# A transformer step on one core: choices and ranks moved in the last three steps, early loads, expert weights rounded in a ring of four

## The reference

```python
# x: 64 images of 2 x 104 x 104; 169 tokens of 128 features per image
y = conv(normed, W, strides=(8, 8)); y = y.reshape(B, E, -1).transpose(0, 2, 1)
...
q_prime = exp(q @ proj.T); k_prime = exp(k @ proj.T)        # 8 heads, 64 features
context = einsum('bhmf,bhmd->bhfd', k_prime, v)
out = einsum('bhnf,bhfd->bhnd', q_prime, context) / (q_prime @ k_prime.sum()  + 1e-6)
...
topv, topi = top_k(x @ Wg, 2); w = softmax(topv)            # 2 of 8 experts per token
for e in range(8):
    h = silu(x @ W[e]) * (x @ V[e])                         # 128 -> 512
    y = y + gw[..., e:e+1] * (h @ W2[e])                    # 512 -> 128
h = h + y
```

## Time and profile before

| | |
|---|---|
| median of 3 runs | 1195.61 us (1195.36 to 1195.7) |
| the profiled execution: its own time, its span | 1192.06 us, 1190.3 us |
| PE busy | 1087.2 us, 91% of the span |
| DVE busy | 857.5 us, 72% |
| ACT busy | 567.8 us, 48% |
| POOL busy | 605.4 us, 51% |
| last steps (32 to 34) and hand-over to the experts | about 652 to 721 us |
| expert loop | about 721 to 1190 us |

### The profile page before, as it was taken

How to read it: one execution, slowest core, us unless ns; L and a number is a source line. 1 busy time by engine, 2 the same in 40 slices (tenths; PEclk the granted TensorE clock), 3 DMA queues, 4 the chain that set the end, 5 groups by cost and what they waited for, 6 DMA issues and landing times.

```text
span 1190.3 us, 30102 instructions
## 1 busy us (share of the span) xinstructions
PE 1087.2 (91%) x8568; PEld 920.2 (77%) x8569; DVE 857.5 (72%) x3329; ACT 567.8 (48%) x1318; POOL 605.4 (51%) x666
## 2 busy tenths in 40 slices
PE   3699999999999999999999627999999999999994
PEld 2567777777677776767667427999999999999994
DVE  5458787887887877878776674777777777777772
ACT  3354635436344354363333314555555555555551
POOL 2002535444444545353545452666666666666664
PEclk9899999999999999999999857999999999999998
DMA  8260131210301313010101142444444444444442
GB/s 168 37 189 13 37 73 35 64 45 29 79 28 39 70 31 79 29 34 27 34 26 42 32 131 50 54 57 53 54 55 53 53 54 55 53 55 55 54 54 22
DMA packets 75792, 65.54 MB, mean 55 GB/s; under 512 B 12382, under 2 KB 66718, under 8 KB 75712
## 3 DMA queue, kind: packets, MB, share of 16 engines
q0 software_dynamic: 33024, 25.86, 15.4%
q1 hardware_dynamic: 42496, 38.32, 13.7%
q10 hardware_dynamic: 192, 0.37, 0.2%
HBM read 32.81 MB, written 31.71 MB: 54 GB/s over the span
## 4 chain that ended last, share of the span: by engine, by line
PE 68%; issue 13%; DVE 7%; POOL 3%; SPq 2%; DMA 1%; ACT 1%; POOLq 0%; DVEq 0%; ACTq 0%
PE bank L1256 22%; PE bank L1268 13%; PE bank L583 7%; PE bank L655 4%; PE bank L642 3%; PE bank L537 3%; PE bank L648 3%; PE bank L629 2%; DVE patches L747 2%; DVE xtok L859 2%; PE bank L426 2%; PE bank L1244 2%; PE bank L630 2%; PE bank L631 2%; DVE attn L798 2%
## 5 line engine op out<-in xcount | busy, mean ns | idle before, releaser
L1397 POOL DMA_INDIRECT out_rows<-yo,dest x184 | 302.0, 1641 | 168.7 <-issue 116.5
L1256 PE MATMUL bank<-xT_e,wv 128*128 128x256 f32 x2208 | 289.6, 287 | 0.9 <-DVE xT_e L1348 0.9
L1256 PEld LDWEIGHTS bank<-xT_e,wv 128*128 128x128 f32 x2208 | 272.5, 190 | 1.3 <-DVE xT_e L1348 1.3
L1160 POOL DMA_INDIRECT sorted_rows<-xrow_all,sloti x192 | 189.1, 985 | 75.1 <-issue 54.4
L1326 ACT ACTIVATE sil<-bank 128x256 f32<-128x256 f32 x368 | 141.6, 385 | 160.4 <-PE bank L1256 154.2
L1355 DVE TENSOR_TENSOR hid<-sil,bank 128x256 f32<-128x256 f32 x368 | 154.9, 421 | 85.1 <-ACT sil L1326 77.1
L1268 PE MATMUL bank<-w,hid 128*128 x1472 | 179.5, 275 | 1.0 <-DVE hid L1355 1.0
L1268 PEld LDWEIGHTS bank<-w,hid 128*128 128x128 f32 x1472 | 171.5, 192 | 1.2 <-issue 1.2
L1133 POOL TENSOR_SCALAR vare<-mv 128x3 f32<-128x3 f32 x64 | 12.6, 196 | 302.2 <-issue 249.4
L1311 ACT CAST wv<-wv_all 128x1024 fp32r x92 | 96.3, 1047 | 41.1 <-issue 27.9
L1071 ACT ACTIVATE attn<-bank 128x256 f32<-128x256 f32 x128 | 49.5, 387 | 130.7 <-PE bank L631 130.7
(11 more groups left out here) (189 smaller groups left out, 1845.3 us busy)
## 6 DMA issues: line engine op xcount, KB each, us to landing
xr<-sorted_rows SPq DMA_DIRECT2D x92, 130.0 KB
raw<-in_x SPq DMA_DIRECT2D x64, 84.5 KB
raw<-in_x SPq DMA_DIRECT2D x60, 78.0 KB
out_rows<-attn SPq DMA_DIRECT2D x64, 58.5 KB
sorted_rows<-xrow_all,sloti POOLq DMA_INDIRECT x192, 2.3
out_rows<-yo,dest POOLq DMA_INDIRECT x184
wv_all<-in_L_ffn_W SPq DMA_DIRECT2D x8, 256.0 KB, 5.7
wv_all<-in_L_ffn_V SPq DMA_DIRECT2D x8, 256.0 KB, 5.9
```

Source lines behind the costliest of these rows:

```text
L1160: po.indirect_dma_start(sorted_rows, bass.IndirectOffsetOnAxis(sloti[:, p, j, ch:ch + 1], 0), xrow[:, p, j, ch], None).then_inc(s(f"scatte ...
L1256: q = pe.matmul(bank[fc][:, TT * m:TT * m + TT], wv[:, p, w_, m, cols], xT[:, p, x_], start=(w_ + x_ == 0), stop=(w_ == 1))
L1397: po.indirect_dma_start(out, bass.IndirectOffsetOnAxis(dest[:, p, a:a + 1], 0), yo[:, p, a], None, compute_op=ALU.add).then_inc(s(f"added{ ...
```

## The change

Four edits are made together.

1. `lo_high`, `lo_low` and `wl_all` are gone. The ring `wv` has four places in place of two. ACT rounds the weights of tile `t+2` while tile `t` is worked on, and DVE subtracts (1024 columns at once) the low part of tile `t+1` as the first thing of tile `t`. The loop body has four tiles, in 22 passes.
2. In the steps 32 to 34, `choose` and the two rank matmuls stand ahead of the place at which they stood; the normalised rows (`normal_rows`) stand behind the denominators in the steps 32 and 33. POOL scatters all six of a pair ahead of the root in step 32, and four of them in step 33.
3. SP issues the eight loads of `w2` in step 32, ahead of that step's output rows. The padding blocks are shared out: SP issues those of the even experts, ACT those of the odd ones. SP loads the first two row numbers to registers before it waits for the scatters.
4. ACT does one small Silu, whose result nobody reads, when the last exponential is done.

```diff
+                if n == NPAIR:
+                    sp.wait_ge(s("conv_done"), NPAIR)
+                    for e in range(E):
+                        expert_sync(sp, "down_weights", e)
...
-            for e in range(E):
-                r = sp.value_load(ends[0:1, e:e + 1], min_val=e * CAP, max_val=e * CAP + NTOK)
-                sp.dma_start(sorted_rows[bass.ds(r, TT)].rearrange("(a p) n -> p a n", a=2), pad).then_inc(s("pads_out"), 16)
+            pad_ends(sp, range(0, E, 2))
...
+            sp.wait_ge(s("table_ready"), 2)
+            first = [expert_sync(sp, "row_number", t) for t in range(2)]
...
+                if d and not a and not b:
+                    rank()
...
+                if b and d and not a:
+                    rank()
...
-                if not a:
-                    lo_low(ve, n - NPAIR, 0)
-                if d:
+                def normal_rows():
...
+                if d and a:
+                    normal_rows()
+                if n > NPAIR:
+                    choose(md)
                 if c:
                     ve.wait_ge(s("d8_done"), mc + 1)
...
+                if d and not a:
+                    normal_rows()
+                if n == NPAIR:
+                    choose(md)
...
+            ac.wait_ge(s("egap_ready"), NPAIR)
+            ac.activation(esum_silu[:], egap[:], ACT.Silu)
+            ac.wait_ge(s("ends_ready"), 1)
+            pad_ends(ac, range(1, E, 2))
...
+                before_root = {NPAIR: 3, NPAIR + 1: 2}.get(n, 1)
...
-                    scatter((0,))
+                    scatter(range(before_root))
...
-                    scatter((1, 2))
+                    scatter(range(before_root, NCH))
...
-    wv = sb("wv", [128, 2, 2, 2, F], F32R)
-    wl_all = sb("wl_all", [128, E, 2, F])
+    wv = sb("wv", [128, 4, 2, 2, F], F32R)
...
+            with eng.Fori(0, (NT - 4) // 4) as i:
+                for u in range(4):
+                    step(4 * i + 2 + u, 2 * i + 1 + u // 2, u % 2, (2 + u) % 4, True, True, True)
...
-                    high_w(t + 1, 1 - p)
+                    if more2:
+                        high_w(t + 2, (w + 2) % 4)
...
-            at_least(ve, s("hv_done"), 4 * (t - 1))
-            ve.tensor_copy(wv[:, p, 1].rearrange("p m n -> p (m n)"),
-                           wl_all[:, bass.ds(e, 1)].rearrange("p e m n -> p (e m n)")).then_inc(s("w_low"), 1)
+            ve.wait_ge(s("w_high"), t + 1)
+            at_least(ve, s("hv_done"), 4 * (t - 3))
+            ve.tensor_tensor(wv[:, w, 1].rearrange("p m n -> p (m n)"),
+                             wv_all[:, bass.ds(e, 1)].rearrange("p e m n -> p (e m n)"),
+                             wv[:, w, 0].rearrange("p m n -> p (m n)").bitcast(F32), ALU.subtract).then_inc(s("w_low"), 1)
...
+            if more:
+                low_w(t + 1, (w + 1) % 4)
             product(t, p, 0)
             product(t, p, 1)
             if more:
                 low_x(t + 1, 1 - p)
-                low_w(t + 1, 1 - p)
```

More of the change, by code:

```diff
@@ L399, in _ @@
                 sp.wait_ge(s(f"scattered{q}"), NPAIR // 2 * 96)
-            sp.wait_ge(s("table_ready"), 2)
-            expert_sync(sp, "rows", 0)
+            expert_sync(sp, "rows", first)
         @block.tensor
@@ L508, in q_feature, with rank @@
                              lambda a_: xT[:, pb, a_, 0:QW]).then_inc(s("q_mm"), 1)
+                def rank():
+                    pe.wait_ge(s("before_step"), NCH * (md + 1))
+                    if a:
+                        pe.wait_ge(s("ln1_x"), n + 1)
+                    else:
+                        pe.wait_ge(s("h2_copied"), n - 2)
+                        pe.wait_ge(s("logit_read"), n - 2)
+                    pe.matmul(ranks[:, :], whole_numbers[:, 0], before[:].rearrange("p c e -> p (c e)"), start=True, stop=False)
+                    pe.matmul(ranks[:, 0:NCH * E], whole_numbers[:, 1], both[:].rearrange("p c e -> p (c e)"), start=False, stop=True
+                              ).then_inc(s("rank_done"), 1)
                 if n == 1:
@@ L586, in step @@
                             t.then_inc(s("out_done"), 1)
[L587 to L594, removed]
-                        pe.matmul(ranks[:, 0:NCH * E], whole_numbers[:, 1], both[:].rearrange("p c e -> p (c e)"), start=False, stop=True
-                                  ).then_inc(s("rank_done"), 1)
+                    if a and d and i == 1:
+                        rank()
                 if b:
@@ L851, in step @@
                     normalise(1)
-                if not a:
-                    lo_low(ve, n - NPAIR, 1)
                 front(0)
@@ L1224, in sync, with row_number, rows @@
             return
-        def rows(t, h, p):
-            r = sp.value_load(table[0:1, bass.ds(t, 1), 0], min_val=0, max_val=E * CAP)
+        def row_number(t):
+            return sp.value_load(table[0:1, bass.ds(t, 1), 0], min_val=0, max_val=E * CAP)
+        if what == "row_number":
+            return row_number(e)
+        def rows(t, h, p, r=None):
+            if r is None:
+                r = row_number(t)
             at_least(sp, s("tok_t"), t - 1)
@@ L1231, in rows @@
                          ).then_inc(s(f"rows_in{p}"), 16)
-        rows(0, 0, 0)
-        rows(1, 0, 1)
+        rows(0, 0, 0, e[0])
+        rows(1, 0, 1, e[1])
         with sp.Fori(0, (NT - 2) // 2) as i:
@@ L1245, in turn, with hidden @@
             q.then_inc(s("tok_t"), 1)
-        def hidden(t, p, fc):
+        def hidden(t, p, w, fc):
             if fc == 0:
@@ L1270, in down, with step @@
             q.then_inc(s("y_done"), 1)
-        def step(t, h, p, more, prev):
-            hidden(t, p, 0)
-            hidden(t, p, 1)
+        def step(t, h, p, w, more, prev, more2):
+            hidden(t, p, w, 0)
+            hidden(t, p, w, 1)
             if more:
```

69 lines of the change are left out of this document (23 added, 46 removed).

## The result

The changed kernel takes 1182.69 us (median of 4 runs, 1181.96 to 1184.87) against 1195.65 us for the kernel before on the same chip (4 runs, 1195.36 to 1196.97): a ratio of 0.9892, with a 95% interval of 0.9877 to 0.9908. That is 13.0 us less; 14.7 were forecast.

A forecast was written before the change was run, and what follows sets the result against it. The end was held to move with the time of the first tile's transposes and the 4.88 us of an expert tile. Terms 5.0 + 2.0 + 3.7 + 4.0 = 14.7 us took 1195.6 to 1180.9 us, range 1175 to 1187.

The forecast's parts named there:

- Step 32: From the denominators to the transposes: without the subtractions and DVE's wait for ACT's rounding, transposes start 5.0 us sooner.
- the full clock: PE in step 32: shorter idle pieces keep the clock up, so the output matmuls take 2.56 us, not 4.11.
- the low clock: Step 32 rival: outputs stay at 4.11 us, gain 2.9; with scatters landing late too, 1184.7 us, chance 0.2.
- Step 33: Best experts to outputs 8.0 us instead of 9.01, outputs to transposes 0.8 instead of 1.8: together 2.0 us sooner.
- Step 34: Best experts to last addresses: three pairs of subtractions go, 8.09 us becomes 4.4, a gain of 3.7 us.
- POOL: Scatters and copies keep up without margin, no term; rival that POOL or padding holds the hand-over: 1187 to 1189, chance 0.09.
- The hand-over: Last addresses to first tile's rows landed: 17.0 us becomes 13.0, with the last scatter landing in 3.0; gain 4.0 us.
- The loop: Expert loop: tiles stay at 4.88 us despite about 0.6 us more DVE work each, so 0 gained or lost.
- fetch was needed on each pass: Expert loop rival: the body grown from 11 to 22 KB is fetched on all 22 passes, 46 us, 1227 us; chance 0.05.
- margin of 1.1 us on DVE: Expert loop: the low part of x ends at 907.9 us, and PE asks for it at 909.0.
- The second rival: Expert loop: DVE becomes a tile's bound; a subtraction twice as long loses 0.2 us or more a tile, 1199; chance 0.03.

The follow-up runs named there:

- ring_only: Kernel before with only the first edit (weights rounded in the expert loop, ring of four, no subtractions in the last steps): 1189.58 us, ratio 0.9945.
- no_moves: Changed kernel with choices, ranks, normalised rows and POOL's scatters at their old places (second edit undone): 1183.77 us, ratio 0.9892.
- moves_only: Kernel before with only the second edit (choices, ranks, normalised rows and scatters moved; subtractions stay): 1290.74 against 1288.38 us, ratio 1.0031.
- pads_after: Changed kernel with all padding issued by SP behind the first two row loads, waited for ahead of the third: 1260.31 against 1263.39 us, ratio 0.9965.
- pads_between: Changed kernel with padding behind the first two row loads, in pieces of three, three and two blocks between the next loads: ratio 0.9927.
- no_silu: Changed kernel without ACT's early Silu: 1250.44 us against 1263.39 us for the kernel before on that chip, ratio 0.9896.
- after_again: Changed kernel once more with no edit, on the third chip, against the kernel before there: ratio 0.9943.
- pads_one_queue: Changed kernel with all eight padding blocks issued by SP, none by ACT: 1183.99 us, ratio 0.9891.
- extra_1024: Changed kernel with DVE's whole 1024-column subtraction done twice in each tile: 1310.53 us, one run.

## Why the prediction was right, and where it was not

**Step 32 (5.0 forecast, 4.75 measured).** Right in size, and wrong on the reason for a part of it. I held that PE would keep the full clock, since its first wait became short. It did not: after the wait of 2.05 us the k features ran at 0.63 us each, as they did before the change once the clock had fallen. But they had risen to 0.40 again by 664.13, ahead of the outputs, which took 2.46. The granted clock by stretches of 5 us:

```profile
660.00:665.00 5.00, 4.57 (x14) 3.32 (x15) 4.50 (x20) 1.20 (x2) 2.92 (x6) 0.66 0.90 268
665.00:670.00 5.00, 5.00 (x27) 3.38 (x26) 2.44 (x12) 0.69 (x2) 1.80 (x2) 1.00 0.77 207
```

At 0.66 it was as low as before in the first stretch. PE was busy for 4.57 of these 5 us. The second stretch is where they differ; in the kernel before:

```profile
665.00:670.00 5.00, 3.76 (x17) 3.76 (x17) 4.44 (x21) 0.68 (x2) 0.00 (x0) 0.71 0.00 0
```

Nor was the first wait what decided. `ring_only` keeps it as long as before, 3.55 us, and runs all nine matmuls of the k features at 0.63 us, and still its outputs take 2.46 us (so do those of `no_moves`, after the same wait). In `moves_only`, whose denominators stand early but whose subtractions stay, they take 4.18. First two rows of `ring_only`, then one of `moves_only`:

```profile
661.04 0.94 PE L506 MATMUL bank<-rparts,pick_head 104*128 104x340 f32 x2 [3.55 <-DVE rparts L845]
...
666.99 2.46 PE L601 MATMUL bank<-attn 128*128 128x169 f32 x16
```

```profile
763.56 4.18 PE L598 MATMUL bank<-attn 128*128 128x169 f32 x16 [2.11 <-DVE attn L805]
```

What goes with slow outputs is a second wait right ahead of them, 1.91 us in the kernel before and 2.11 in `moves_only`. Without it PE works through from the broadcast, with no pause above 0.43 us, and the clock is back in time. That second wait went with the subtractions, so the 1.5 us of the outputs belong to the first edit. That they came out as forecast, for a reason that didn't hold, is luck.

The outputs started at A + 10.5, where I had put A + 10.1. DVE's last `normalise` ended at 665.19 + 0.51 = 665.70, which is A + 10.1; the 0.4 is PE's own work, which ran late. The 2.9 that I gave for the low clock isn't worked out: 4.11 - 2.56 alone makes it 3.5.

**Step 33 (2.0, 1.90).** 682.49 - 674.62 = 7.87 us to the outputs, for a forecast of 8.0; 0.79 us between outputs and transposes, for 0.8. After the transposes the best experts came 0.25 us later than before.

**Step 34 (3.7, 3.71).** I gave all of it to the three pairs of subtractions. Taking them out brings 8.09 to 4.94 (`ring_only`), 3.15 us. The other 0.56 comes from the moves (4.94 and 4.93 without them, 4.38 with them), and only once the subtractions are gone: `moves_only` has 8.07. The sum was right and its split was not.

**POOL.** It kept up: six scatters of pair 29 from 667.90 on, the root 1.03 us after the sixth was issued, and the copies of the last pair done at 695.8, 0.2 us ahead of the last addresses. In `no_moves` the last scatter is issued 9.24 us after the addresses instead of 7.56, so in the old order POOL would have been late.

**The hand-over (4.0, 2.21) is the term that was mis-sized, and the landing of the last scatter is the step that failed.** Issue of the last scatter 7.56 us after the addresses (7.6), load issued 0.22 us after the landing (0.35), load 2.1 (2.08): all as worked out. For the landing I had "2.3 to 4.7 us" and took 3.0, "nearer to the median". It took 4.91. `pads_after` and `pads_between` show the cause: with no padding beside it the same scatter lands in 2.35 and 2.30 us, where with it the same chips have 4.53 (`no_silu`) and 4.85 (`after_again`).

The mistake was in reading. Its median of 2.3 is that of all 192 scatters, nearly all of them with no padding beside them. The six that did have padding beside them landed in 3.9 to 4.7 us in the kernel before, and these were the rows to take. Two queues for the padding aren't needed to make the last one late: with one (`pads_one_queue`) it took 4.6. In the kernel before it took 3.9, but nobody waited for it, as the padding ended later. With 4.91 in place of 3.0 the sum is 12.8.

**The loop (0, 0.1).** No fetch was needed on each pass: one packet of the instruction queue in 400 us, which is some 20 passes. My reading of the rule in the Trainium skill ("Runtime: NRT & Kernel Launch", Instruction fetch mechanics) was too quick. It speaks of a window of two pages; of 16 KiB each, they make 32 KiB, more than the 22 KB that I estimated for the body. So a stall didn't follow from it, unless the body lies across three pages, and this run tells neither for nor against the rule or the 128 KiB. The margin of 1.1 us on DVE was not there as I had worked it out; the subtraction of 1024 columns took 1.22 us. The second rival's price was too low for the same reason: I gave 0.2 us a tile for a subtraction of twice the length, and `extra_1024`, which does it twice, lost 0.70.

**The attribution.** My sum counts the four edits as if each gave its own part. The runs say otherwise. The ring alone gives 5.7 to 6.6 us, the moves alone no gain that could be seen (beside the other edits some 2 us in the traces), and without the early `w2` 3.1 us of the whole are lost again in the trace. What DVE gives, SP's list takes, unless it is shortened too.

**Open.** What the moves are worth in timed runs. Why the changed kernel gains only half as much on the third chip. What makes the clock fall and come back in step 32. Whether `pads_between` is faster by the 2.5 us that its trace shows: the chip it ran on scatters by more than that. Padding ahead of the scatters for tiles that aren't full, which the two kernels need for all inputs, wasn't tried.

## What to carry to other kernels

When a stage ends in a hand-over, list for each engine and queue when its part is done, not only for the one waited for: taking 4 us from the last makes the next one the last, here SP's issues and then the landing of a DMA. Take the price of a transfer from the stretch in which it will run, not from a median over the whole kernel: beside other traffic the same scatter took twice as long. And to see how much an off-path engine can still take, double its operation in a run. The distance of one result from its use (1.1 us here) overstates it, and so does the sum of its waits (0.93 a tile): 0.5 could be used.

## What the runs showed of the hardware that was not expected

An indirect scatter of 128 rows of 520 bytes landed in 2.3 us with no padding beside it, in 3.3 to 4.6 us beside padding blocks of 130 KB from one queue, and in 4.2 to 6.2 us beside the same eight blocks from two. Four microseconds of the changed kernel (two queues), then four of `pads_one_queue`; the last two columns are the mean busy share of the DMA engines and the GB/s:

```profile
700.00:704.00 4.00, 0.00 (x0) 0.00 (x0) 3.48 (x12) 0.56 (x1) 3.08 (x4) 0.50 1.17 158
```

```profile
702.00:706.00 4.00, 0.00 (x0) 0.00 (x0) 3.48 (x12) 0.35 (x1) 3.08 (x4) 0.50 0.54 156
```

The same bytes are moved in both, with twice the time of packets in the first. (The share adds up the time of packets, so it can pass 1.) So in this stretch the second queue moved nothing more; packets only took longer, those of the scatters too. The short rows aren't the reason by themselves: both stretches have them. Why two queues do this isn't shown.

The chips of the second and third group took 5.7 and 7.8% longer for the kernel before (1263.39 and 1288.38 against 1195.65 us). The expert loop did not slow down there: in `no_silu` it took 483.8 us from the last addresses to the end, in the changed kernel 484.1. The unrolled step loop did, in irregular steps, for instance:

```profile
172.44 1.73 PE L625 MATMUL bank<-ident_gate,h1T 128*128 128x136 f32 x6 [3.27 <-DVE h1T L899]
196.78 0.96 PE L625 MATMUL bank<-ident_gate,h1T 128*128 128x136 f32 x6 [1.87 <-DVE h1T L899]
```

In the trace of the kernel before the same wait sums up to 6.8 us in nine places from 60 to 640 us, 0.8 us each. What holds the engines there was not found out.
